# A graph-network kernel on one core: the column-number table of three wide comparisons moved from SBUF into a PSUM bank

## The chip, the core and the metric

The kernel runs on one core of one Trainium2 chip. A core has a matrix engine (PE, with its weight loads shown apart as PEld), a vector engine (DVE), a scalar engine (ACT), a general engine (POOL, also GpSimd) and a queue engine (SP); each works through its own list of instructions in order, and semaphores are the only ties between the lists. Data lie in SBUF, in PSUM (eight banks of 512 fp32 numbers per partition, written by PE, readable and writable by DVE and ACT) and in HBM. The metric is the time of one execution on the device in microseconds (us). The kernel before took 3636.62 us (median of 2 runs, 3635.95 to 3637.29).

## The reference

Four graph-network layers in a row on 6250 nodes of 128 features and 206250 edges sorted by target node. Only what bears on the change is shown:

```
def _L0_gnn_ref(x, edge_index, edge_attr, W, edge_w, b):
    src, dst = (edge_index[0], edge_index[1])
    xw = x @ W
    ew = edge_attr @ edge_w
    msg = xw[src] * ew
    out = jax.ops.segment_sum(msg, dst, num_segments=x.shape[0])
    return out + b
# layers 1 to 3: gather x[src], scale by degrees, segment_sum over dst, dense product
x = _layernorm(x + _L0_gnn_ref(...)); x = _layernorm(x + _L1_gnn_ref(...))
x = _layernorm(x + _L2_gnn_ref(...)); x = _layernorm(x + _L3_gnn_ref(...))
```

Layer 0 needs one row of `xw` per edge, multiplied by that edge's own product, and summed by target node. Layers 1 to 3 multiply node features by an adjacency matrix, which the kernel builds while layer 0 runs.

## The kernel before, in words

**Stages.** A short preparation computes `xw` and stores it in HBM. Then comes the **gather stage**, an unrolled loop of NH = 202 steps `n`, each for 8 tiles of 128 edges. Last come the dense layers, in which SP loads the stored adjacency matrix and PE multiplies.

**One step of the gather stage, engine by engine.**

- POOL issues 8 indirect DMAs (L563), each fetching 128 rows of `xw` into one of NG = 4 buffers of `gath`. Before step `n` it waits until step `n - 4` has been multiplied (`s_msg`). Every eighth step it issues one more indirect DMA (L547) for the edges of 256 target nodes.
- DVE, in this order: every eighth step `split_slots` (L631 to L642) turns edge words into pairs of small numbers; `hots(n - 4)` makes two comparison tables (L652: 16 tiles of 128 columns, L654: 16 tiles of 98 columns); `window_add(n - 1)` (L663) adds a PSUM result into `yT`; two multiplications (L677) form the messages from PSUM and `gath`; `window_hot(n + 1)` (L619) makes the comparison table of the next step, 8 tiles of 64 columns. Each comparison is a tensor_tensor `is_equal` of a table of column numbers with one number per tile and partition, broadcast.
- PE, in this order: every eighth step `turn_slots` (two transposes, L937); `a_products(n - 4)` (16 small products, L947, which ACT evicts from two PSUM banks); the message products (8 products, 16 records, L970) into bank 2 or 3 by turns; the edge products of the next step (2 products, 4 records, L930) into banks 0 and 1; `out_degrees` (4 products, L953).
- ACT copies the turned pairs (L1105) every eighth step and evicts four pairs of `a_products` per step (L1099). SP loads edge attributes and stores the adjacency blocks.

**Names.** `cols_key` and `cols_p` are the fp16 tables of column numbers (98 and 128 wide), `cols_pf` the fp32 one (128 wide); all lie in SBUF. `lokeyT` and `rel` are the numbers they are compared with, also in SBUF. `PB` is PSUM as eight banks; bank 7 holds the two turned places until ACT has copied them. The POOL instructions that make the tables are L529 to L531.

Of the kernel before, what the change touches and what calls it, by code (L numbers as in the profile page):

```python
# [14 lines left out]
F16 = mybir.dt.float16  # L15
# [9 lines left out]
P = 128  # L25
NB = -(-N // P)
NP = NB * P
T8 = 8
# [39 lines left out]
def build(nc, xT_d, x_d, ea_d, src_d, dst_d, next_d, edges_d, firstq_d, first16_d, half_d, w_d, vec_d, out_d):  # L68
    ctx = ExitStack()
    with ctx:  # L70
# [99 lines left out]
        first_edge = sb("first_edge", [P, NPB], I32)  # L170
        below = sb("below", [P, NPB, 3])
        pair_deg = sb("pair_deg", [P, NPB, 2])
        cols_key = sb("cols_key", [P, KW], F16)
        cols_p = sb("cols_p", [P, P], F16)
        cols_pf = sb("cols_pf", [P, P])
        flags = sb("flags", [P, 3])
        off_f = sb("off_f", [P, 1])
# [12 lines left out]
        g_block = msg[:, 0, :]  # L190

        PB = ctx.enter_context(nc.psum_tensor("pb", [P, 8, 512], F32))

        s_in = {n: sem("in_" + n) for n in ("w", "edge_w", "xT0", "xT1", "vecs", "src", "edges", "firsts", "rows", "x")}
        s_const = sem("consts_made")
# [323 lines left out]
        @block.gpsimd  # L519
        def _(pool):  # L520
            nc.gpsimd.iota(pair_dst[:, :], [[2 * P, NPB]], base=0, channel_multiplier=2, allow_small_or_imprecise_dtypes=True)
            nc.gpsimd.memset(edge_w[:, :, :], 0.0).then_inc(s_const, 1)
            nc.gpsimd.memset(ident[:, :], 0.0)
            nc.gpsimd.memset(x[:, NB - 1, :], 0.0).then_inc(s_const, 1)
            pool.wait_ge(s_const, 2)
            nc.gpsimd.affine_select(out=ident[:, :], in_=ident[:, :], compare_op=ALU.not_equal, fill=1.0,
                                    base=0, pattern=[[-1, P]], channel_multiplier=1)
            nc.gpsimd.memset(ones[:, :], 1.0)
            nc.gpsimd.iota(cols_key[:, :], [[1, NB], [NB, 2]], base=0, channel_multiplier=0, allow_small_or_imprecise_dtypes=True)  # L529
            nc.gpsimd.iota(cols_p[:, :], [[1, P]], base=0, channel_multiplier=0, allow_small_or_imprecise_dtypes=True)  # L530
            nc.gpsimd.iota(cols_pf[:, :], [[1, P]], base=0, channel_multiplier=0, allow_small_or_imprecise_dtypes=True)  # L531
            nc.gpsimd.iota(pair_key[:, :], [[KW * P, NPB]], base=0, channel_multiplier=KW, allow_small_or_imprecise_dtypes=True)
            nc.gpsimd.memset(flags[:, :], 0.0)
            nc.gpsimd.memset(g_deg[:, :, :], 0.0)
            nc.gpsimd.memset(eps_ln[:, 1:2], 1e-5)
            nc.gpsimd.memset(eps_ln[:, 3:4], 0.0)
            nc.gpsimd.iota(valid[:, :], [[0, 1]], base=0, channel_multiplier=1, allow_small_or_imprecise_dtypes=True).then_inc(s_const, 1)

            for b in range(NPB):
                if b % 5 == 0:  # L540
                    pool.wait_ge(s_q, b // 5 + 1)
                    pool.sem_inc(s_seen, 1)
                nc.gpsimd.indirect_dma_start(first16_i[:, b, :], None, first16_d,  # L543
                                             bass.IndirectOffsetOnAxis(ap=first_q[:, b:b + 1], axis=0)).then_inc(s_f16, 16)

            def slots_in(b):
                nc.gpsimd.indirect_dma_start(slots[:, b, :, :].rearrange("p e k -> p (e k)"), None, edges_d,  # L547
                                             bass.IndirectOffsetOnAxis(ap=first_edge[:, b:b + 1], axis=0)).then_inc(s_slot[b % 2], 16)

            pool.wait_ge(s_tab, 5)  # L550
            pool.wait_ge(s_rowxw, 2 * NT)
            pool.sem_inc(s_seen, 1)
            slots_in(0)
            pool.wait_ge(s_in["src"], 16)
            for h in range(2):
                pool.wait_ge(s_rowst[h], 16 * TURNS[h])
            pool.sem_inc(s_seen, 1)
            for n in range(NH):
                if n >= NG:
                    pool.wait_ge(s_msg, 2 * (n - NG) + 2)  # L560
                    pool.sem_inc(s_seen, 1)
                for t in range(n * T8, min(n * T8 + T8, ET)):
                    nc.gpsimd.indirect_dma_start(gath[:, T8 * (n % NG) + t % T8, :], None, xw_d,  # L563
                                                 bass.IndirectOffsetOnAxis(ap=src_i[:, t:t + 1], axis=0)).then_inc(s_gath[n % NG], 16)
                if n % BL == BL // 2 and n // BL + 1 < NPB:
                    slots_in(n // BL + 1)
            g_off = off(pool)
            general_pool(pool, 0, g_off)
            for k, bias in ((1, B_L1), (2, B_L2), (3, None)):
                Wk = s_walk[k]  # L570
                if k == 1:

                    pool.wait_ge(s_prep, NPB)

                def residual(t, s, p):
                    pool.wait_ge(Wk[f"xn{s}"], p + 1)
                    if k < 3:
                        nc.gpsimd.tensor_tensor(blocks(y, t), xn[s], vecs[:, bias, :].unsqueeze(1).broadcast_to([P, BT, D]), ALU.add).then_inc(Wk[f"yb{s}"], 1)  # L578
                    else:
                        pool.dma_start(x3_d[bass.ds(t * (BT * P), BT * P), :].rearrange("(b p) f -> p b f", p=P), xn[s]).then_inc(Wk[f"st{s}"], 16)  # L580

                walk(pool, residual)
                general_pool(pool, k, g_off)

            pool.wait_ge(s_x3, 16)
            nc.gpsimd.tensor_tensor(x3b, x3b, vecs[:, BN_BETA, :].unsqueeze(1).broadcast_to([P, NB, D]), ALU.add).then_inc(s_bn_pool, 1)  # L586

        @block.vector
        def _(v):
# [23 lines left out]
            nc.vector.tensor_scalar(first_edge[:, :], before_16[:, :], float(2 * FE), None, ALU.mult).then_inc(s_tab, 1)  # L613
            v.wait_ge(s_const, 3)
            nc.vector.tensor_copy(ident16[:, :], ident[:, :]).then_inc(s_tab, 1)  # L615

            def window_hot(n):
                at_tile = T8 * (n % 2)
                nc.vector.tensor_tensor(hot_win[:, at_tile:at_tile + T8, :], cols_pf[:, 0:WIN].unsqueeze(1).broadcast_to([P, T8, WIN]),  # L619
                                        rel[:, n * T8:n * T8 + T8].unsqueeze(2).broadcast_to([P, T8, WIN]), ALU.is_equal).then_inc(s_hotw, 1)  # L620

            cuts = [NPB + 1]
# [23 lines left out]
            def hots(j):  # L646
                b, c = j // BL, j % BL * NPR
                if j >= 2:
                    v.wait_ge(s_amm, GA * (j - 1))
                v.wait_ge(s_lk, b + 1)  # L650
                at_pair = NPR * (j % 2)
                nc.vector.tensor_tensor(hot_lo[:, at_pair:at_pair + NPR, :], cols_p[:, :].unsqueeze(1).broadcast_to([P, NPR, P]),  # L652
                                        lokeyT[:, b, c:c + NPR].unsqueeze(2).broadcast_to([P, NPR, P]), ALU.is_equal)
                nc.vector.tensor_tensor(hot_key[:, at_pair:at_pair + NPR, :], cols_key[:, :].unsqueeze(1).broadcast_to([P, NPR, KW]),  # L654
                                        lokeyT[:, b, P + c:P + c + NPR].unsqueeze(2).broadcast_to([P, NPR, KW]), ALU.is_equal).then_inc(s_hot, 1)

            def window_add(n):
# [254 lines left out]
        def _(pe):  # L912
# [18 lines left out]

            def turn_slots(b):
                pe.wait_ge(s_prep, b + 1)
                if b > 0:
                    pe.wait_ge(s_lk, b)
                for k in range(2):
                    last = nc.tensor.transpose(PB[:, 7, k * P:k * P + P], lo_key[:, k, :], ident[:, :])  # L937
                last.then_inc(s_tp, 1)

            def a_products(j):  # L940
# [19 lines left out]
            for n in range(NH):  # L960
                if n % BL == 2 and n // BL < NPB:
                    turn_slots(n // BL)
                if 0 <= n - LAG < NA:
                    a_products(n - LAG)
                pe.wait_ge(s_msg, 2 * n + 2)
                pe.wait_ge(s_hotw, n + 1)
                if n >= 2:
                    pe.wait_ge(s_add, n - 1)
                for t in range(T8):
                    last = nc.tensor.matmul(PB[:, 2 + n % 2, 0:WIN], msg[:, T8 * (n % 2) + t, :], hot_win[:, T8 * (n % 2) + t, :], start=(t == 0), stop=(t == T8 - 1))  # L970
                last.then_inc(s_win, 1)
                if n + 1 < NH:
                    edge_products(n + 1)
                if 0 <= n - LAG - 1 < NA:
                    out_degrees(n - LAG - 1)
            pe.wait_ge(s_off, 5)
            pe.wait_ge(s_lk, NPB)
            nc.tensor.matmul(PB[:, 7, 0:3], ones[:, :], flags[:, :], start=True, stop=True).then_inc(s_off, 1)
            pe.wait_ge(s_add, NH)
            g_off = off(pe)  # L980
# [96 lines left out]
        def _(act):  # L1077
# [24 lines left out]
            for n in range(NH):  # L1102
                if n % BL == 2 and n // BL < NPB:
                    act.wait_ge(s_tp, n // BL + 1)
                    nc.scalar.copy(lokeyT[:, n // BL, :], PB[:, 7, 0:2 * P]).then_inc(s_lk, 1)  # L1105
                if 0 <= n - LAG < NA:
                    evict(n - LAG)

# [134 lines left out]
```

## Time and profile before

| what | value |
|---|---|
| time, median of 2 runs | 3636.62 us |
| the profiled execution's own time | 3642.16 us |
| its span | 3639.8 us |
| PE busy | 2578.6 us (71%) |
| POOL busy | 2024.1 us (56%) |
| DVE busy | 1574.8 us (43%) |
| ACT busy | 530.3 us (15%) |
| indirect DMAs of the gather stage on POOL | 1612, from 58.8 to 2499.1 us |

The page gives busy times over the whole span. The gather stage fills about the first 2500 us and the dense layers the rest, and the two have different limits, so a share of the whole says little on either. In the lists, "idle before, releaser" tells how long an engine stood idle ahead of a group's instructions and what ended that; "issue" is time in which it waited for nothing that the profile shows. A matrix product of fp32 numbers shows as two records.

### The profile page before, as it was taken

What the parts mean: (1) busy time and instruction counts of PE and PEld (TensorE: products, weight loads), DVE (VectorE), ACT (ScalarE), POOL (GpSimd) and SP (SyncE); (2) the same over time, 40 slices, a digit from 0 to 9 for tenths busy, and PEclk for the clock granted to TensorE, in tenths of its full rate; (3) what the DMA queues carried; (4) which work ended last, traced back from release to release, by engine and by line L of the source; (5) the groups of instructions that cost most, each with busy time, mean ns of one, the idle gap of its engine ahead of it and who ended that gap; (6) DMA issues with size and microseconds to landing.
All of it is one profiled execution on the core that took longest, in us unless ns stands there. A gap on an engine that the chain in (4) does not pass through costs nothing.

```text
span 3639.8 us, 35592 instructions
## 1 busy us (share of the span) xinstructions
PE 2578.6 (71%) x12818; PEld 1594.3 (44%) x12818; DVE 1574.8 (43%) x2392; ACT 530.3 (15%) x1141; POOL 2024.1 (56%) x1703
## 2 busy tenths in 40 slices
PE   3566666766666666666667676765799899879980
PEld 2344444444444444444444444443444444545540
DVE  3455555455545454545454545454311311231136
ACT  0111111111111111111111111110200300111112
POOL 6777777777777777777777777773100200000001
PEclk7777777777777777777777777776899999889995
DMA  5222222222222222222222222226177577627641
GB/s 177 72 83 81 86 82 86 81 87 86 78 85 86 82 85 83 85 86 81 83 83 82 86 82 85 84 83 178 73 289 295 223 295 294 239 106 282 270 163 35
DMA packets 215777, 462.28 MB, mean 127 GB/s; under 512 B 43877, under 2 KB 84042, under 8 KB 215386
## 3 DMA queue, kind: packets, MB, share of 16 engines
q1 hardware_dynamic: 159358, 344.17, 25.4%
q0 software_dynamic: 54480, 112.65, 12.3%
q10 hardware_dynamic: 1804, 3.72, 0.3%
q8 instruction: 77, 1.26, 0.2%
q14 instruction: 58, 0.48, 0.0%
HBM read 372.09 MB, written 88.32 MB: 126 GB/s over the span
## 4 chain that ended last, share of the span: by engine, by line
POOL 51%; PE 25%; issue 16%; DVE 5%; another core or an unknown queue 1%; DMA 1%; ACT 1%; DVEq 0%; ACTq 0%; POOLq 0%; SPq 0%
POOL big L563 49%; PE pb L1032 11%; PE pb L1033 11%; PE pb L1007 1%; PE pb L1041 1%; POOL big L543 1%; POOL y L547 1%; DMA big<-at 0%; DVE y L886 0%; ACT tmp L1133 0%; PE pb L970 0%; DVE tmp L770 0%; DVE big L652 0%; PE pb L1057 0%
## 5 line engine op out<-in xcount | busy, mean ns | idle before, releaser
L563 POOL DMA_INDIRECT big<-xw,big x1612 | 1910.4, 1185 | 501.0 <-issue 490.9
L970 PE MATMUL pb<-big 128*128 128x64 f32 x3232 | 635.1, 378 | 638.8 <-DVE big L677 618.3
L970 PEld LDWEIGHTS pb<-big 128*128 128x128 f32 x3232 | 599.8, 286 | 671.6 <-DVE big L677 649.9
L677 DVE TENSOR_TENSOR big<-pb,big 128x512 f32<-128x512 f32 x404 | 261.3, 687 | 1103.5 <-DMA big<-xw,big 1059.0
L1032 PE MATMUL pb<-big,yT 128*128 128x512 f16 (+1 forms) x1911 | 688.0, 368 | 23.1 <-DMA big<-at 17.5
L930 PE MATMUL pb<-big 128*128 128x512 f32 x808 | 672.7, 982 | 24.4 <-DVE ident L615 24.4
L1033 PE MATMUL pb<-big,yT 128*128 128x512 f16 (+1 forms) x1911 | 687.8, 368 | 0.0
L1099 ACT CAST tmp<-pb 128x392 f16<-128x392 f32 x784 | 349.8, 488 | 1740.9 <-PE pb L947 1056.1
L652 DVE TENSOR_TENSOR big<-cols_p,big 128x2048 f16<-128x2048 f16 x196 | 447.9, 2285 | 0.8
L947 PE MATMUL pb<-big 128*128 128x98 f16 x3136 | 247.2, 212 | 173.7 <-ACT tmp L1099 80.8
L654 DVE TENSOR_TENSOR big<-cols_key,big 128x1568 f16<-128x1568 f16 x196 | 349.6, 1784 | 0.0
L930 PEld LDWEIGHTS pb<-big 128*128 128x128 f32 x808 | 235.3, 320 | 224.6 <-issue 224.6
L947 PEld LDWEIGHTS pb<-big 128*128 128x128 f16 x3136 | 176.2, 100 | 267.1 <-issue 124.7
L1032 PEld LDWEIGHTS pb<-big,yT 128*128 128x128 f16 x1911 | 187.5, 98 | 230.2 <-issue 26.7
L1033 PEld LDWEIGHTS pb<-big,yT 128*128 128x128 f16 x1911 | 187.4, 98 | 206.7 <-issue 2.5
L578 POOL TENSOR_TENSOR y<-tmp,vecs 128x896 f32 (+1 forms) x14 | 35.0, 2506 | 361.8 <-ACT tmp L1133 361.8
L828 DVE SCALAR_TENSOR_TENSOR y<-pb,small,y 128x128 f32 (+1 forms) x98 | 26.7, 344 | 460.5 <-PE pb L1041 460.5
L586 POOL TENSOR_TENSOR big<-big,vecs 128x6272 f32<-128x6272 f32 x1 | 13.4, 13387 | 341.5 <-DMA big<-x 341.5
L953 PEld LDWEIGHTS pb<-tmp,ident 128*128 128x128 f16 x784 | 91.7, 117 | 226.1 <-issue 205.2
L953 PE MATMUL pb<-tmp,ident 128*128 128x392 f16 x784 | 190.1, 371 | 0.0
L580 POOL DMA_DIRECT2D x<-tmp x7 | 6.7, 952 | 301.2 <-ACT tmp L1133 291.4
L619 DVE TENSOR_TENSOR big<-cols_pf,big 128x512 f32<-128x512 f32 x202 | 138.4, 685 | 0.0
(145 smaller groups left out, 1008.0 us busy)
## 6 DMA issues: line engine op xcount, KB each, us to landing
big<-at SPq DMA_DIRECT2D x36, 6272.0 KB, 18.0
at<-tmp SPq DMA_DIRECT2D x196, 392.0 KB
big<-xw,big POOLq DMA_INDIRECT x1612
big<-in_ea SPq DMA_DIRECT2D x202, 64.0 KB
big<-at SPq DMA_DIRECT2D x3, 1568.0 KB, 6.6
xw<-big SPq DMA_DIRECT2D x7, 448.0 KB
x<-tmp POOLq DMA_DIRECT2D x7, 448.0 KB, 7.3
out<-tmp SPq DMA_DIRECT2D x6, 448.0 KB, 3.0
```

The lines of the kernel that those rows point to most:

```text
L563: nc.gpsimd.indirect_dma_start(gath[:, T8 * (n % NG) + t % T8, :], None, xw_d, bass.IndirectOffsetOnAxis(ap=src_i[:, t:t + 1], axis=0)).th ...
L619: nc.vector.tensor_tensor(hot_win[:, at_tile:at_tile + T8, :], cols_pf[:, 0:WIN].unsqueeze(1).broadcast_to([P, T8, WIN]), rel[:, n * T8:n ...
L652: nc.vector.tensor_tensor(hot_lo[:, at_pair:at_pair + NPR, :], cols_p[:, :].unsqueeze(1).broadcast_to([P, NPR, P]), lokeyT[:, b, c:c + NPR ...
L654: nc.vector.tensor_tensor(hot_key[:, at_pair:at_pair + NPR, :], cols_key[:, :].unsqueeze(1).broadcast_to([P, NPR, KW]), lokeyT[:, b, P + c ...
L677: nc.vector.tensor_tensor(msg[:, T8 * (n % 2) + 4 * q:T8 * (n % 2) + 4 * q + 4, :], PB[:, q, :].rearrange("p (t f) -> p t f", f=D), gath[: ...
L930: nc.tensor.matmul(PB[:, q, :], ea[:, n % NG, :], edge_w[:, 4 * q:4 * q + 4, :], start=True, stop=True).then_inc(s_ew, 1)
L947: last = nc.tensor.matmul(PB[:, 4 + g % 2, i * KW:i * KW + KW], hot_lo[:, at_pair, :], hot_key[:, at_pair, :], start=True, stop=True)
L953: last = nc.tensor.matmul(PB[:, 6, 0:NB * T8], ident16[:, :], stage[:, j % 2, :].rearrange("p (h d) -> p h d", d=SN)[:, :, g * T8:g * T8 + ...
L970: last = nc.tensor.matmul(PB[:, 2 + n % 2, 0:WIN], msg[:, T8 * (n % 2) + t, :], hot_win[:, T8 * (n % 2) + t, :], start=(t == 0), stop=(t = ...
L1032: nc.tensor.matmul(PB[:, c, 0:n], parts_v[0][:, b, :], piece, start=(b == 0), stop=False)
L1033: last = nc.tensor.matmul(PB[:, c, 0:n], parts_v[1][:, b, :], piece, start=False, stop=(b == NB - 1))
L1099: nc.scalar.copy(stage[:, j % 2, :].rearrange("p (h d) -> p h d", d=SN)[:, :, c:c + 2 * GP].rearrange("p h (i a) -> p h i a", a=2), PB[:, ...
```

## The change

The two fp16 tables become one fp32 table in PSUM, 226 columns of bank 7: DVE copies `cols_pf` and `cols_key` (now fp32) there once, before the first step. The three comparisons read it. The general path, which these inputs don't take, still reads `cols_pf` in SBUF. The turned places lie in columns 64 to 319 of bank 2 instead, beside the message products' 64 columns. The waits are changed with that: `turn_slots` waits for the addition that last read bank 2, the message products of every eighth step wait for ACT's copy of the turned places, and the three-column product at the end, which goes to bank 7, waits until all comparisons are done.

```diff
-        cols_key = sb("cols_key", [P, KW], F16)
-        cols_p = sb("cols_p", [P, P], F16)
+        cols_key = sb("cols_key", [P, KW])
         cols_pf = sb("cols_pf", [P, P])
...
         PB = ctx.enter_context(nc.psum_tensor("pb", [P, 8, 512], F32))
+        cols = PB[:, 7, 0:P + KW]
...
-            nc.gpsimd.iota(cols_p[:, :], [[1, P]], base=0, channel_multiplier=0, allow_small_or_imprecise_dtypes=True)
...
             nc.vector.tensor_copy(ident16[:, :], ident[:, :]).then_inc(s_tab, 1)
+            nc.vector.tensor_copy(cols[:, 0:P], cols_pf[:, :])
+            nc.vector.tensor_copy(cols[:, P:P + KW], cols_key[:, :]).then_inc(s_tab, 1)
+            v.wait_ge(s_tab, 7)
...
-                nc.vector.tensor_tensor(hot_win[:, at_tile:at_tile + T8, :], cols_pf[:, 0:WIN].unsqueeze(1).broadcast_to([P, T8, WIN]),
+                nc.vector.tensor_tensor(hot_win[:, at_tile:at_tile + T8, :], cols[:, 0:WIN].unsqueeze(1).broadcast_to([P, T8, WIN]),
...
-                nc.vector.tensor_tensor(hot_lo[:, at_pair:at_pair + NPR, :], cols_p[:, :].unsqueeze(1).broadcast_to([P, NPR, P]),
+                nc.vector.tensor_tensor(hot_lo[:, at_pair:at_pair + NPR, :], cols[:, 0:P].unsqueeze(1).broadcast_to([P, NPR, P]),
...
-                nc.vector.tensor_tensor(hot_key[:, at_pair:at_pair + NPR, :], cols_key[:, :].unsqueeze(1).broadcast_to([P, NPR, KW]),
+                nc.vector.tensor_tensor(hot_key[:, at_pair:at_pair + NPR, :], cols[:, P:P + KW].unsqueeze(1).broadcast_to([P, NPR, KW]),
...
             def turn_slots(b):
                 pe.wait_ge(s_prep, b + 1)
-                if b > 0:
-                    pe.wait_ge(s_lk, b)
+                pe.wait_ge(s_add, b * BL + 1)
                 for k in range(2):
-                    last = nc.tensor.transpose(PB[:, 7, k * P:k * P + P], lo_key[:, k, :], ident[:, :])
+                    last = nc.tensor.transpose(PB[:, 2, WIN + k * P:WIN + k * P + P], lo_key[:, k, :], ident[:, :])
...
                     pe.wait_ge(s_add, n - 1)
+                if n % BL == 2 and n // BL < NPB:
+                    pe.wait_ge(s_lk, n // BL + 1)
...
-            pe.wait_ge(s_lk, NPB)
+            pe.wait_ge(s_hotw, NH)
+            pe.wait_ge(s_hot, NA)
...
-                    nc.scalar.copy(lokeyT[:, n // BL, :], PB[:, 7, 0:2 * P]).then_inc(s_lk, 1)
+                    nc.scalar.copy(lokeyT[:, n // BL, :], PB[:, 2, WIN:WIN + 2 * P]).then_inc(s_lk, 1)
```

## Rows read from the trace of the kernel before

**Rows 1.** The page: the span in 40 slices, POOL busy and TensorE clock, in tenths

```profile
POOL 6777777777777777777777777773100200000001
PEclk7777777777777777777777777776899999889995
```

**Rows 2.** The page: chain that ended last, shares of the span by line

```profile
POOL big L563 49%; PE pb L1032 11%; PE pb L1033 11%; PE pb L1007 1%; PE pb L1041 1%; POOL big L543 1%; POOL y L547 1%; DMA big<-at 0%; DVE y L886 0%; ACT tmp L1133 0%; PE pb L970 0%; DVE tmp L770 0%; DVE big L652 0%; PE pb L1057 0%
```

**Rows 3.** The page: costliest groups; busy us, mean ns of one, idle before

```profile
L563 POOL DMA_INDIRECT big<-xw,big x1612 | 1910.4, 1185 | 501.0 <-issue 490.9
...
L677 DVE TENSOR_TENSOR big<-pb,big 128x512 f32<-128x512 f32 x404 | 261.3, 687 | 1103.5 <-DMA big<-xw,big 1059.0
...
L652 DVE TENSOR_TENSOR big<-cols_p,big 128x2048 f16<-128x2048 f16 x196 | 447.9, 2285 | 0.8
...
L654 DVE TENSOR_TENSOR big<-cols_key,big 128x1568 f16<-128x1568 f16 x196 | 349.6, 1784 | 0.0
...
L619 DVE TENSOR_TENSOR big<-cols_pf,big 128x512 f32<-128x512 f32 x202 | 138.4, 685 | 0.0
```

**Rows 4.** Line L563: duration ns min/median/max, first and last start

```profile
L563 POOL DMA_INDIRECT big<-xw,big x1612: 942/947/2964, 58.8 to 2499.1; - x180
```

**Rows 5.** Timeline, an issue with DVE idle: start us, us, what [idle before]

```profile
60.05 0.95 POOL L563 DMA_INDIRECT big<-xw,big  x1 [0.30 <-issue]
```

**Rows 6.** Timeline of one step in the middle, POOL and DVE

```profile
1504.68 1.29 DVE L677 TENSOR_TENSOR big<-pb,big 128x512 f32<-128x512 f32 x2 [6.14 <-DMA big<-xw,big]
1505.79 0.95 POOL L563 DMA_INDIRECT big<-xw,big  x1 [0.31 <-issue]
1505.88 0.68 DVE L619 TENSOR_TENSOR big<-cols_pf,big 128x512 f32<-128x512 f32 x1
...
1506.48 2.29 DVE L652 TENSOR_TENSOR big<-cols_p,big 128x2048 f16<-128x2048 f16 x1
1507.04 2.55 POOL L563 DMA_INDIRECT big<-xw,big  x1 [0.30 <-issue]
1508.68 1.78 DVE L654 TENSOR_TENSOR big<-cols_key,big 128x1568 f16<-128x1568 f16 x1
...
1509.89 1.40 POOL L563 DMA_INDIRECT big<-xw,big  x1 [0.30 <-issue]
1510.39 0.21 DVE L663 TENSOR_TENSOR yT<-yT,pb 128x64 f32 x1
```

**Rows 7.** Timeline of PE: a step at the low clock, a step at the high one

```profile
1107.26 3.67 PE L970 MATMUL pb<-big 128*128 128x64 f32 x16 [6.37 <-DVE big L677]
...
1116.70 0.74 PE L947 MATMUL pb<-big 128*128 128x98 f16 x8 [0.47 <-issue]
...
156.21 1.96 PE L970 MATMUL pb<-big 128*128 128x64 f32 x16
...
162.78 1.96 PE L970 MATMUL pb<-big 128*128 128x64 f32 x16
```

**Rows 8.** Stretches: PE, PEld, DVE, ACT, POOL busy, then clock, DMA share, GB/s

```profile
137.00:170.00 33.00, 27.07 (x188) 18.04 (x188) 32.00 (x32) 7.78 (x18) 27.08 (x20) 0.95 0.32 99
...
1000.00:1500.00 500.00, 338.83 (x1677) 224.27 (x1678) 256.41 (x304) 76.92 (x173) 398.15 (x335) 0.73 0.29 84
```

**Rows 9.** Groups by shape: busy us, mean ns of one, idle before

```profile
L547 POOL DMA_INDIRECT y<-in_edges,first_edge x25 | 23.7, 948 | 13.2 <-issue 7.3 <-DVE ident L615 5.9
...
L1105 ACT CAST big<-pb 128x256 f16<-128x256 f32 x25 | 9.3, 373 | 353.0 <-PE pb L937 181.1 <-remote 151.5 <-issue 20.4
...
L636 DVE SCALAR_TENSOR_TENSOR tmp<-y,tmp 128x128 f32<-128x128 int32 x25 | 7.8, 313 | 0.0
L698 DVE TENSOR_TENSOR x<-x,vecs 128x896 f32<-128x896 f32 x7 | 7.6, 1085 | 0.0
```

**Rows 10.** Timeline of the start, DVE's last preparation and first multiplication

```profile
56.62 0.22 DVE L615 CAST ident<-ident 128x128 f16<-128x128 f32 x1
...
70.21 1.29 DVE L677 TENSOR_TENSOR big<-pb,big 128x512 f32<-128x512 f32 x2 [12.77 <-DMA big<-xw,big]
```

## The prediction, made before the changed kernel had run

> **What bounds the kernel now.** I read four views in this order. The page's slices show two regimes: POOL is busy at seven tenths for about 28 of 40 slices and then nearly silent, with the TensorE clock at 0.7 to 0.8 first and 0.9 after [rows 1]. The chain of waits puts 49% of the span on one POOL line, L563, and 11% on each of the two dense products [rows 2]. So the gather stage ends when POOL has issued its 1612 indirect DMAs, and only that stage is touched by the change. The costliest groups then give the shape of the bound: L563 is busy 1910.4 us, 1185 ns a piece, and the idle time ahead of it is 490.9 us of "issue", 0.30 us a piece, with almost nothing that another engine releases. DVE, for its part, stands idle for 1059.0 us until gathered rows land [rows 3]. Nobody holds POOL up by a semaphore; it is slow by itself.
>
> The line's own view says how slow. The median issue is 947 ns and the shortest 942, while the mean is 1185 and the longest 2964 [rows 4]. With DVE idle an issue takes 0.95 us and the next comes 0.30 us later [rows 5], so eight of them would be 10.0 us a step. The stage takes (2499.1 - 58.8) / 201.5 = 12.1 us a step [rows 4] (the last step has 4 issues).
>
> The timeline of a step shows where 2.1 us go [rows 6]. The issue of 1507.04 begins inside the comparison L652 (1506.48 to 1508.77) and takes 2.55 us: it ends at 1509.59, 0.82 us after the comparison. The one of 1509.89 begins inside L654 (ending 1510.46) and takes 1.40: it ends at 1511.29, 0.83 after. The one of 1505.79 begins inside the second multiplication of L677 (1504.68 to 1505.97) and takes 0.95: nothing is added. L677 reads one operand in PSUM and one in SBUF; L652 and L654 read both in SBUF. My reading: an issue that needs SBUF while DVE reads two SBUF operands stands still until DVE is done, then needs its last 0.82 us.
>
> **The change, part by part.**
>
> 1. *Three comparisons read their table in PSUM.* With one SBUF operand left they are of L677's kind, so I take the whole added time away. 1612 issues at the median 0.947 are 1526.6 us; measured are 1910.4 [rows 3, 4]; excess 383.8 us. Not all of it goes. Two-SBUF instructions that the change leaves are the seven additions L698 (1.09 us each) and the pair steps of `split_slots` (25 times 0.31 for L636, with one more like it beside it) [rows 9]. An issue caught by one of the seven loses at most 1.09 + 0.82 - 0.95 = 0.96 us, seven of them 6.7 us; the short ones lose at most 0.2, fifty of them 10. As most won't fall so, I keep 6 us and take **378 us** off. Bounds: 384 if nothing is left, 367 if all fall badly.
>
> 2. *What the comparisons themselves cost.* The nearest row is L677 against L619, both 128x512 fp32, the one from PSUM and the other from SBUF alone: 687 and 685 ns [rows 3]. L652 and L654 in fp16 lie on L619's line, (2285 - 685) / (2048 - 512) = 1.04 ns an element, so fp16 buys nothing that an fp32 table would lose. I take 2 ns each, off the path: DVE waits 6.14 us a step for rows to land [rows 6]. Without that cover 594 comparisons would cost 1.2 us.
> [...]
>
> 3. *PE's bank 2.* `turn_slots` now waits for the addition of step 8b, which DVE's list has ahead of the split that it waited for already: nothing. The message products of step 8b + 2 wait for ACT's copy, 0.37 us [rows 9]; between the two PE does `a_products`, whose ACT evictions come behind that copy in ACT's list, so only the first of the 25 (no `a_products` yet) may pay 0.4 us, at a step where POOL is four buffers ahead. The last product waits for comparisons that were done before the message products ahead of it: nothing.
>
> 4. *Start.* One iota on POOL goes, ahead of a wait for DVE: nothing. Two copies on DVE come in; L615 is the nearest, 0.22 us [rows 10], so 0.5 us, ahead of a multiplication that waits 12.77 us for its rows [rows 10]. With no cover, 0.5.
>
> **Does POOL stay the bound?** At 10.0 us a step others come close.
> DVE: 1.29 + 0.68 + 2.29 + 1.78 + 0.21 = 6.25 us [rows 6]. Far.
> PE: its list closes on itself, since every product of a step needs the one before. [...] POOL needs a buffer back only after three further steps, 30 us, which evens single slow steps out.
>
> **The sum.** The profiled execution's own time is 3642.16, 5.5 over the median of the runs, 3636.62. 3642.2 - 378 = 3264; the same against the median is **3259 us**, 10.4% less. The dense layers are not touched.
>
> **The rivals.**
>
> *A. PE becomes the bound (0.07).* If the clock stays low, a PE step costs 10.2 to 10.6 us (the upper end where `out_degrees` is slow as well), 0.2 to 0.6 above POOL's, times 196: 39 to 118 us given back, 3300 to 3375. [...]
>
> *B. The port is not the cause, or PSUM doesn't free it (0.04).* The two long comparisons are also the longest DVE instructions and write the most. If writing holds POOL up, nothing changes: 3637. Against it: L677 writes as well, and adds nothing [rows 6].
> [...]
>
> *C. DVE becomes the bound, and the kernel slower (0.02).* If reading a broadcast table in PSUM slows the three comparisons by a factor r, DVE's step is 1.50 + 4.75 r. It passes POOL's 10.0 at r = 1.8 and today's 12.1 at r = 2.2; at r = 3 it is 15.8, 3.7 above today's times 196, some 4360 us. Nothing speaks for it but that no row has an fp32 PSUM operand beside an fp16 one or with a repeated column range; L677 speaks against it.
>
> *D. Half the gain (0.03).* The comparisons still block for a part, or gathers at a steady 10.0 us a step meet slower landings: half of 378 is 3448.
>
> **How the numbers follow.** Forecast 0.84. Its own range is 3252 (384 off) to 3272 (367 off, and a few us of clock in the dense layers either way), widened by a slow PE step here and there. With the lower part of A the range is 3245 to 3310; outside lie B, C, D, most of A. About 2% is what a measurement of this kernel can tell from no change: all but B and C are faster by more. Faster 0.94, same 0.04, slower 0.02.
>
> **What the changed profile would show.** Right: L563's mean within 10 ns of 947, its longest under 2 us, its last start at 2499 - 378 = 2121 us, a step of 10.0 us, the three comparisons within 10 ns of now, DVE's wait for rows about 4 us a step. Steps above 10.0 with message products that start right behind `a_products`, and a clock near 0.5, would be A. Issues that still end 0.82 us after a comparison would be B. Comparisons of double length would be C. The forecast is wrong too if POOL shows idle time released by L677, the sign that a buffer comes back late.

## The result: slower by 3.8%, and the profile after

| | before | after |
|---|---|---|
| median | 3636.62 us | 3775.78 us (3774.11 to 3777.45) |
| ratio to before | | 1.0383, interval 1.0338 to 1.0427 |
| span of the profiled execution | 3639.8 us | 3772.0 us |
| POOL busy | 2024.1 us | 1640.0 us |
| last indirect DMA of the stage starts at | 2499.1 us | 2618.9 us |

Forecast were 3259 us and a last issue at 2121 us. POOL lost 384 us of work, and the stage became 120 us longer. The span grew by 132.2 us: 119.8 until the last issue, 12.4 behind it.

The page of the changed kernel, in the order of parts 2, 4 and 5, answers to [rows 1], [rows 2] and [rows 3]:

```profile
POOL 6566666556556556655655655564100100000001
PEclk6666677677666767667776766677699999979995
...
PE 44%; another core or an unknown queue 31%; issue 12%; ACT 7%; DVE 4%; DMA 1%; ACTq 1%; DVEq 0%; POOL 0%; SPq 0%; POOLq 0%
...
L562 POOL DMA_INDIRECT big<-xw,big x1612 | 1526.6, 947 | 1005.0 <-DVE big L679 554.5
...
L665 DVE TENSOR_TENSOR yT<-yT,pb 128x64 f32 x202 | 43.6, 216 | 1141.1 <-remote 1105.9
L654 DVE TENSOR_TENSOR big<-pb,big 128x2048 f16<-128x2048 f32 x196 | 447.1, 2281 | 0.8
L679 DVE TENSOR_TENSOR big<-pb,big 128x512 f32<-128x512 f32 x404 | 269.2, 687 | 200.8 <-PE pb L932 153.2
L656 DVE TENSOR_TENSOR big<-pb,big 128x1568 f16<-128x1568 f32 x196 | 348.7, 1779 | 0.0
```

The issue L562 fell from 1185 to 947 ns, as forecast, and the comparisons cost what they did. But POOL now stands idle for 554.5 us until a multiplication gives a buffer back (10.1 us before, in the full row of this line), the multiplication no longer waits for rows, and DVE spends 1105.9 us ahead of the addition L665, released by "remote". POOL's share of the chain that ended last is 0%; 31% of it is "another core or an unknown queue". Both words say that the view found no instruction whose end explains the release. There is one core, so that is a thing to look into, and the timeline shows it. A step of the changed kernel, all engines:

```profile
1491.94 0.53 PE L948 MATMUL pb<-big 128*128 128x98 f16 x8
...
1492.40 0.49 ACT L1103 CAST tmp<-pb 128x392 f16<-128x392 f32 x1 [6.87 <-PE pb L954]
...
1492.94 0.35 PE L948 MATMUL pb<-big 128*128 128x98 f16 x4 [0.47 <-issue]
...
1494.87 0.48 ACT L1103 CAST tmp<-pb 128x392 f16<-128x392 f32 x1 [1.98 <-remote]
...
1495.41 0.35 PE L948 MATMUL pb<-big 128*128 128x98 f16 x4 [2.11 <-issue]
...
1495.60 1.96 PE L973 MATMUL pb<-big 128*128 128x64 f32 x16
...
1497.40 3.61 PE L932 MATMUL pb<-big 128*128 128x512 f32 x4
...
1498.39 0.49 ACT L1103 CAST tmp<-pb 128x392 f16<-128x392 f32 x1 [3.04 <-remote]
...
1502.67 0.48 ACT L1103 CAST tmp<-pb 128x392 f16<-128x392 f32 x1 [3.79 <-PE pb L948]
...
1504.31 0.94 POOL L562 DMA_INDIRECT big<-xw,big  x1 [0.30 <-issue]
1508.51 0.33 SPq L465 DMA_DIRECT2D big<-in_ea  x1
1508.53 0.22 DVE L665 TENSOR_TENSOR yT<-yT,pb 128x64 f32 x1 [11.87 <-remote]
1508.67 1.28 DVE L679 TENSOR_TENSOR big<-pb,big 128x512 f32<-128x512 f32 x2
1508.71 0.87 ACT L1103 CAST tmp<-pb 128x392 f16<-128x392 f32 x2 [5.56 <-remote]
1509.25 0.90 PE L948 MATMUL pb<-big 128*128 128x98 f16 x8 [5.01 <-ACT tmp L1103]
...
1510.73 0.94 POOL L562 DMA_INDIRECT big<-xw,big  x1 [5.48 <-DVE big L679]
```

The addition L665 waits for the message products L973. Those end at 1497.56; the addition starts at 1508.53, 11.0 us later, with DVE idle. SP waits for the edge products L932, which end at 1501.01, and goes on at 1508.51. ACT goes on at 1508.71. So three engines that wait for PE alone, for products that ended at different times, are released within 0.2 us of each other. By the profile the products are done (a product's end is modelled there, but the products behind L973 had started too); what is late, then, is their **completion signal**. The trace has a record of semaphore updates besides, and it agrees: the update by the message products stands at 1508.41, those by the edge products at 1508.45 and 1508.49, while DVE's update for its next multiplication stands at 1509.36, right at that instruction's end.

The addition's late signal (1508.41) arrives 3.2 us after POOL's last issue ends (1505.25), and POOL had stopped because its four buffers were full: it waits for the multiplication, which is behind the addition on DVE, which waits for the signal.

ACT's copies show what happens before POOL stops. The four copies of this step start at 1492.40, 1494.87, 1498.39 and 1502.67, which is 0.1, 2.4, 5.1 and 6.9 us after the ends of their products, while POOL was issuing without a pause. So signals do come through while POOL issues, but each later than the one before.

POOL therefore issues for two steps (20 us), stands for 5.5, and begins again: 12.7 us a step on average ((2618.9 - 58.5) / 201.5), against 12.1 before.

**The sign was in the trace before.** Its start has a stretch in which no comparison blocks POOL yet, steps 0 to 5. The timeline of the kernel before, there:

```profile
86.94 3.67 PE L970 MATMUL pb<-big 128*128 128x64 f32 x16 [8.39 <-DVE big L677]
...
118.85 0.94 POOL L563 DMA_INDIRECT big<-xw,big  x1 [0.30 <-issue]
...
126.23 0.22 DVE L663 TENSOR_TENSOR yT<-yT,pb 128x64 f32 x1 [36.79 <-remote]
...
129.63 0.94 POOL L563 DMA_INDIRECT big<-xw,big  x1 [9.83 <-DVE big L677]
```

The message products of step 1 end at 90.6, and their addition starts 35.6 us later, after POOL had run out of buffers; its last issue had ended 6.4 us before (119.79). I read these rows for the start alone and took the wait for one of its transfers. Nor was every signal prompt later on, when the comparisons did block POOL. In the middle of the stage before the change:

```profile
960.30 2.00 PE L970 MATMUL pb<-big 128*128 128x64 f32 x16 [1.92 <-DVE big L677]
...
969.24 0.95 POOL L563 DMA_INDIRECT big<-xw,big  x1 [0.30 <-issue]
...
969.86 0.22 DVE L663 TENSOR_TENSOR yT<-yT,pb 128x64 f32 x1 [2.99 <-remote]
```

The addition starts 7.6 us after the products' end, and POOL is issuing then, so an arriving signal needs no full stop of POOL. Such waits are few there: the addition waited 65.7 us for "remote" in the whole run, against 1105.9 after the change.

### The profile page after: what moved, and what is told of

The parts are those of the page before. It is cut to its first block, busy times and chain, and to the rows that moved or that the text cites. A ratio compares the mean times of both kernels' runs of the same rounds, so it can differ in the third digit from the quotient of the medians.

```text
span 3772.0 us, 35619 instructions
## 1 busy us (share of the span) xinstructions
PE 2520.3 (67%) x12818; PEld 1563.0 (41%) x12818; DVE 1574.8 (42%) x2394; ACT 541.0 (14%) x1141; POOL 1640.0 (43%) x1702
## 4 chain that ended last, share of the span: by engine, by line
PE 44%; another core or an unknown queue 31%; issue 12%; ACT 7%; DVE 4%; DMA 1%; ACTq 1%; DVEq 0%; POOL 0%; SPq 0%; POOLq 0%
PE pb L1036 10%; PE pb L1037 10%; PE pb L932 7%; PE pb L973 7%; ACT tmp L1103 6%; PE pb L948 5%; PE pb L954 2%; PE pb L1011 1%; PE pb L1045 1%; ACT tmp L1137 1%; DMA big<-at 0%; DVE y L888 0%; DVE tmp L772 0%; PE pb L1061 0%
## 5 line engine op out<-in xcount | busy, mean ns | idle before, releaser
L562 POOL DMA_INDIRECT big<-xw,big x1612 | 1526.6, 947 | 1005.0 <-DVE big L679 554.5
L948 PE MATMUL pb<-big 128*128 128x98 f16 x3136 | 301.2, 230 | 950.3 <-ACT tmp L1103 489.0
L1103 ACT CAST tmp<-pb 128x392 f16<-128x392 f32 x784 | 361.3, 487 | 2073.6 <-remote 1115.6
L948 PEld LDWEIGHTS pb<-big 128*128 128x128 f16 x3136 | 199.5, 108 | 1069.9 <-ACT tmp L1103 534.9
L973 PE MATMUL pb<-big 128*128 128x64 f32 x3232 | 600.0, 363 | 55.1 <-DVE big L679 54.8
L932 PE MATMUL pb<-big 128*128 128x512 f32 x808 | 619.8, 912 | 24.3 <-DVE ident L614 24.3
L973 PEld LDWEIGHTS pb<-big 128*128 128x128 f32 x3232 | 572.1, 274 | 66.1 <-DVE big L679 61.5
L665 DVE TENSOR_TENSOR yT<-yT,pb 128x64 f32 x202 | 43.6, 216 | 1141.1 <-remote 1105.9
L654 DVE TENSOR_TENSOR big<-pb,big 128x2048 f16<-128x2048 f32 x196 | 447.1, 2281 | 0.8
L656 DVE TENSOR_TENSOR big<-pb,big 128x1568 f16<-128x1568 f32 x196 | 348.7, 1779 | 0.0
L932 PEld LDWEIGHTS pb<-big 128*128 128x128 f32 x808 | 213.7, 291 | 201.1 <-issue 201.1
```

The costliest lines, as they stand in the source:

```text
L665: nc.vector.tensor_tensor(where, where, PB[:, 2 + n % 2, 0:WIN], ALU.add).then_inc(s_add, 1)
L932: nc.tensor.matmul(PB[:, q, :], ea[:, n % NG, :], edge_w[:, 4 * q:4 * q + 4, :], start=True, stop=True).then_inc(s_ew, 1)
L948: last = nc.tensor.matmul(PB[:, 4 + g % 2, i * KW:i * KW + KW], hot_lo[:, at_pair, :], hot_key[:, at_pair, :], start=True, stop=True)
L1103: nc.scalar.copy(stage[:, j % 2, :].rearrange("p (h d) -> p h d", d=SN)[:, :, c:c + 2 * GP].rearrange("p h (i a) -> p h i a", a=2), PB[:, ...
```

## The experiments

Theory 1, formed from these rows: **PE's completion signals arrive late while POOL issues indirect DMAs without a break. The two-SBUF comparisons used to make the breaks**, one of about 1.6 us and one of about 0.45 us a step (2.55 and 1.40 us less the usual 0.95 [rows 6]), and the change took them away. Theory 2: the shared bank 2, or the new waits, cost the time. Theory 3: reading the table in PSUM delays PE's signals.

### First group: which part, which cause

The edits below are abridged. `undo_table`, the changed kernel with the three comparisons on SBUF again:

```diff
-  hot_win <- cols[:, 0:WIN];  hot_lo <- cols[:, 0:P];     hot_key <- cols[:, P:P + KW]
+  hot_win <- cols_pf[:, 0:WIN]; hot_lo <- cols_pf[:, :];  hot_key <- cols_key[:, :]
```

> The changed kernel, but the three comparisons read their tables in SBUF again (both fp32); bank 2 for the turned places and the changed waits stay. Theory 1 (PE's completion signals arrive late while POOL issues indirect DMAs without a break; the comparisons used to make the breaks): POOL's mean issue is back at about 1185 ns, PE's signals are prompt again, 3637 us within 10. Theory 2 (a product or a copy in bank 2, or the new waits, cost the time): stays near 3776 or gets worse, since the old issue times come on top. Theory 3 (reading the table in PSUM delays PE's signals) also expects 3637 here.

`short_tables`, from the kernel before, where the two wide comparisons make one tile of 16 (so the adjacency matrix is not the right one):

```diff
+                made = NPR if j < 2 else 1
-  hot_lo[:, at_pair:at_pair + NPR, :] and hot_key[:, at_pair:at_pair + NPR, :]
+  hot_lo[:, at_pair:at_pair + made, :] and hot_key[:, at_pair:at_pair + made, :]
```

> The kernel before, with its tables in SBUF, but the two wide comparisons of each step make one tile of 16 from the third step on (the other 15 keep the first steps' numbers, so the adjacency matrix is not the reference's). DVE neither blocks POOL for long nor reads a table in PSUM. Theory 1: POOL issues without breaks again, PE's signals come late, steps of 10.0 and about 15 us in turn, 3720 to 3800 us although DVE has 3.8 us less to do in a step. Theory 3: no table is read in PSUM, so signals are prompt and POOL sets 10.0 us a step, 3260 us.

`pause_four`, from the changed kernel: four memsets on POOL between the fourth and the fifth gather of a step (`pause_one` has 1 in place of 4):

```diff
                 for t in range(n * T8, min(n * T8 + T8, ET)):
+                    for _ in range(4 if t % T8 in (4,) else 0):
+                        pool.wait_ge(s_idle, paused)
+                        nc.gpsimd.memset(idle_room[:, :], 0.0).then_inc(s_idle, 1)
+                        paused += 1
```

> The changed kernel with one break in POOL's issues per step: four memsets of 384 columns, some 2 us, between the fourth and the fifth gather. Theory 1: the break lets PE's signals through as the comparisons did, a step is 10.0 + 2.0 to 2.3 us, 3620 to 3700 us, less than the changed kernel although POOL has more to do. Theory 3: signals stay late, since the table is still in PSUM, and the added POOL work makes it no faster than 3776.

> The same with one memset, some 0.5 us of break per step. Theory 1 leaves open how long a break must be: if 0.5 us is enough, a step is 10.6 us and the time about 3380 us, better than both kernels; if not, between 3400 and 3776. Theory 3: 3776 or more.

Measured: undo_table 3640.23 us, ratio 1.0006 (0.9994 to 1.0019). short_tables 3774.43 us, 1.0379 (1.0346 to 1.0413). pause_four 3591.15 us, 0.9871 (0.9855 to 0.9888). pause_one 3762.82 us, 1.0349 (1.0332 to 1.0366).

undo_table falls back to the old time with bank 2 and the new waits in place: theory 2 is out. short_tables is the one that separates 1 from 3. It reads no table in PSUM, DVE has 3.5 us less to do in a step (2285 and 1784 ns against 285 and 254 for the short forms), and it is as slow as the changed kernel. The groups of short_tables, its POOL issues and its two comparisons (the means include the two full-size ones of the first steps):

```profile
L563 POOL DMA_INDIRECT big<-xw,big x1612 | 1545.1, 958 | 976.4 <-DVE big L678 528.5 <-issue 447.9
...
L653 DVE TENSOR_TENSOR big<-cols_p,big 128x128 f16<-128x128 f16 (+1 forms) x196 | 59.9, 306 | 0.8
L655 DVE TENSOR_TENSOR big<-cols_key,big 128x98 f16<-128x98 f16 (+1 forms) x196 | 52.9, 270 | 0.0
```

The issues are near 947 ns (958) and the idle time behind full buffers is back at 528.5 us. Theory 3 is out as the cause. pause_four adds work to the engine that sets the pace, and is faster than both kernels, and than the 3620 us that I gave as its lower bound; its groups and one step:

```profile
L569 POOL DMA_INDIRECT big<-xw,big x1612 | 1528.0, 948 | 461.2 <-issue 461.2
...
L567 POOL MEMSET idle_room<- 128x384 f32 x804 | 339.8, 423 | 34.8
...
L672 DVE TENSOR_TENSOR yT<-yT,pb 128x64 f32 x202 | 42.8, 212 | 57.4 <-remote 38.0 <-PE pb L980 19.3
```

```profile
1502.25 3.67 PE L980 MATMUL pb<-big 128*128 128x64 f32 x16 [2.27 <-DVE big L686]
...
1504.29 1.87 POOL L567 MEMSET idle_room<- 128x384 f32 x4
...
1506.31 0.95 POOL L569 DMA_INDIRECT big<-xw,big  x1 [0.16 <-issue]
1506.61 0.21 DVE L672 TENSOR_TENSOR yT<-yT,pb 128x64 f32 x1
```

No idle time is left that a multiplication ends, and the addition waits 57.4 us in all instead of 1141.1. In the step, the message products end at 1505.92 and the addition starts 0.7 us later, as soon as DVE is through with its comparison. POOL is the bound again, at 11.7 us in most steps.

### Second group: how long a break must be

> The changed kernel with two memsets of 384 columns on POOL per step, about 0.85 us more between the fourth and the fifth gather (four gave 1.7 us and 3591 us, one gave 0.29 us and 3763 us). If 0.85 us is enough for PE's signals, a step is 10.0 + 0.85 us and the time 3420 us; if the signals still come late, it lies between 3591 and 3763.

> The same with three memsets, about 1.3 us more. If enough, 10.0 + 1.3 us a step and 3505 us, faster than both kernels and than four memsets; if not, above 3591.

`pause_spread` has one memset where `t % T8 in (1, 3, 5, 7)`, `pause_alternate` has four where `t % (2 * T8) == 4`.

> Four memsets per step again, but one after every second gather, so POOL issues as seldom as with the four in one place, and no break is longer than 0.6 us (0.3 us is usual). If PE's signals need a lower mean rate of issues, 3591 us or less, as with the four together. If they need one long break, they come late in spite of the same POOL work: steps of 15 us among those of 11.2, 3700 us or more.

> Four memsets in one place, but only in every second step. If a 2 us break every 21.7 us lets the waiting signals through in time, a pair of steps takes 21.7 us and the time is about 3430 us; if a break is needed in every step, a step of 15 us comes back for each one without a break, and it is 3650 us or more.

The break is the time from the end of the fourth issue to the start of the fifth, read from each timeline (0.30 us with no memset); the idle time is that of the issue's group which the multiplication ends.

| kernel | longest break in a step | POOL idle for a buffer | time, ratio to before (interval) |
|---|---|---|---|
| changed | 0.30 us | 554.5 us | 3775.78, 1.0383 (1.0338 to 1.0427) |
| pause_one | 0.59 | 465.1 | 3762.82, 1.0349 (1.0332 to 1.0366) |
| pause_two | 1.07 | 342.1 | 3780.61, 1.0369 (1.0322 to 1.0416) |
| pause_three | 1.54 | 198.4 | 3716.03, 1.0211 (1.0160 to 1.0261) |
| pause_four | 2.01 | 0 | 3591.15, 0.9871 (0.9855 to 0.9888) |
| pause_spread | 4 of 0.59 | 253.6 | 3715.62, 1.0192 (1.0163 to 1.0221) |
| pause_alternate | 2.0, every second step | 309.3 | 3802.22, 1.0437 (1.0406 to 1.0468) |

My hope of 3420 or 3505 us with a shorter break failed, and pause_two came out above the 3763 us that I had as its upper end. A break of 0.6 us gains 13 us on the changed kernel and one of 1.1 us nothing, one of 1.5 us gains 60 us, and 2.0 us in every step keeps the signals prompt almost throughout; in every second step it gains nothing. pause_spread has POOL do the same work as pause_four and is 125 us slower, so the rate of issues alone is not what counts. It is 60 us faster than the changed kernel, so neither is the length alone.

### Third group: issues, bytes or landings, and one comparison at a time

> The changed kernel with the widest comparison (16 tiles of 128 columns) reading its table in SBUF again, the other two in PSUM. An issue caught by it stands still for about 1.6 us per step, a break like that of the four memsets, and the 0.45 us that the other wide comparison cost are saved. Theory 1 (a break of that length lets PE's signals through): steps of 11.6 us, 3637 - 196 x 0.45 = 3549 us, faster than both kernels. If the PSUM reads that remain were at fault: 3700 us or more.

> The other way round: only the comparison of 16 tiles of 98 columns reads its table in SBUF. It begins behind the widest one and now an issue that starts inside it stands still for up to 1.7 us, one that starts near its end for 0.1. Theory 1: between 3590 and 3790 us, by how long the break turns out to be; late signals if it is under 1.3 us, prompt ones if it is 1.6.

`narrow_rows` gathers `[..., 0:WIN]` from `xw` seen as rows of 64. `sp_rows`:

```diff
+                if n >= 1 and n - 1 + NG < NH:
+                    sp.wait_ge(s_msg, 2 * n)
+                    rows_in(n - 1 + NG)     # 8 x sp.dma_start(gath tile, 128 rows of xw_d)
...
-                for t in range(n * T8, min(n * T8 + T8, ET)):     # POOL's indirect DMAs
+                for t in range(n * T8, 0):
```

> The changed kernel with gathers that fetch 64 instead of 128 columns from the fifth step on (the other half of each message is an earlier step's, so layer 0 is not the reference's): half the bytes, as many issues. If PE's signals wait for the issues, nothing changes: steps of 10.0 and 15 us in turn, 3760 to 3790 us. If they wait for the gathered bytes on their way, they come earlier: fewer than half of the 15 us steps, under 3700 us.

> The changed kernel with the rows of each step fetched by eight plain DMAs from SP's queue instead of eight indirect ones from POOL (rows in order of place, so layer 0 is not the reference's): the same bytes and landings, no issue on POOL in the stage but one in eight steps. Theory 1 (the issues on POOL hold PE's signals back): signals are prompt, PE or SP sets the step at 7 to 9 us, 2600 to 3000 us. If the landings or the bytes hold them back, signals stay late, as many as in the changed kernel.

Measured: lo_in_sbuf 3621.88 us, 0.9949 (0.9935 to 0.9963); key_in_sbuf 3681.93 us, 1.0118 (1.0101 to 1.0136); narrow_rows 3768.44 us, 1.0356 (1.0324 to 1.0387); sp_rows 2444.17 us, 0.6717.

Half the bytes change nothing, so the bytes are not it; as many gathers landed, so landings are not ruled out by that run. With the issues gone from POOL, as many bytes and eight DMAs landing per step as before, PE's signals are prompt. So neither bytes nor landings as such delay them. But sp_rows changes the engine that issues, its queue and the kind of DMA together, and doesn't tell which of the three counts. The groups of sp_rows and one of its steps:

```profile
L676 DVE TENSOR_TENSOR yT<-yT,pb 128x64 f32 x202 | 42.4, 210 | 11.9 <-PE pb L984 11.9
```

```profile
804.26 1.28 DVE L690 TENSOR_TENSOR big<-pb,big 128x512 f32<-128x512 f32 x2
...
810.08 1.28 DVE L690 TENSOR_TENSOR big<-pb,big 128x512 f32<-128x512 f32 x2
```

A step is 5.8 us, the addition waits 11.9 us in the whole run, and the tables are read in PSUM all the while, which clears them a second time. My 2600 to 3000 us was too high: DVE, not PE or SP, sets that pace; from 200 to 1200 us it is busy for 981.5 of 1000 us, and PE for 891.7. This kernel is no version to use, since it fetches rows in order.

lo_in_sbuf keeps one former break, 1.6 us long (with the usual 0.3, a gap of 1.9, just under that of pause_four), and is 18 us faster than the kernel before, where I had expected 88: 45.1 us of POOL's idle time still wait for a buffer. key_in_sbuf, with the other comparison's break, has 234.6 us. Its issues took 1711.5 us, 0.94 us a step over the 1526.6 of the changed kernel, so that break is shorter.

### Fourth group: the place, and a break on demand

`gate` has POOL do `pool.wait_ge(s_win, n - 1)` between the fourth and the fifth gather; `pause_first` has the four memsets where `t % T8 in (0,)`.

> The changed kernel, where POOL waits between the fourth and the fifth gather of step n until the message products of step n - 2 are signalled. With prompt signals that has long happened and costs nothing; with late ones POOL stops at once, not only when its four buffers are full. If a stop must last some 3.1 us until late signals arrive, as in the changed kernel, whatever the stop is made of, and each step of the stage needs one, a step is 13 us and the time 3800 us or more; if a stop clears the way for a step or two behind it, a pair of steps takes 20.0 + 3.1 us and it is 3560 us.

> The four memsets (3591 us between the fourth and the fifth gather) ahead of the first gather of a step instead. If only the length of the break counts, 3591 us within 15, with steps of 11.7 us. If it counts what PE does during it, the time differs, up to the 3776 us of no break.

Measured: pause_first 3606.62 us, 0.9908 (0.9890 to 0.9926): the place counts 15 us, the length 185. gate 3690.46 us, 1.0145 (1.0127 to 1.0163), 85 us faster than the changed kernel and 99 us slower than pause_four: it lies between my two cases. So stopping POOL until the signal is there gains less than a fixed break does.

## Why the prediction was wrong, step by step

1. **The added time of the issues: right within 6 us.** 1612 issues at 947 ns, 1526.6 us, against 1910.4: 384 us less where I took off 378. undo_table has them at 1182 ns again. The two-SBUF instructions that stay add about 5 us over the median of 944 ns (1526.6 less 1612 x 0.944), where I had kept 6; the longest issue took 2.38 us (the second row below), not under 2: it began inside one of the four flag instructions of steps 6 to 9 (208.19 to 210.02 us), which I had left out, and ended 0.82 us after it, as the issues of [rows 6] do. Rival B falls: the issues took 1185 ns with the three comparisons' tables in SBUF and 947 with them in PSUM, while the two long comparisons took as long either way (point 2). That it is a port for which an issue waits, as that rival's name has it, no run shows.
2. **The comparisons: right.** 2281 and 1779 ns from PSUM, 2285 and 1784 before; none got longer. Rival C falls.
3. **Bank 2 and the waits: right**, at nothing (undo_table 1.0006).
4. **The start: right.** The first issue is at 58.5 instead of 58.8 us.
5. **"Does POOL stay the bound?": this step failed.** I priced PE's step by the times of its products and took for granted that a product's end reaches those who wait for it at once. I counted 30 us of slack from four buffers, but the message products' signals came some 11 us late in every second step, and POOL stood idle for 554.5 us, waiting for buffers. Whether more buffers would have helped was not tried. The stall I removed as a loss was also what kept another path open, and it was the cheaper of the two: 2.05 us a step, against 2.7 for full buffers.
6. Rival A named PE as the next bound for its speed, and that is not what happened: in the changed stage PE is idle for 38% of the time, at a granted clock of 0.70 (the first row below) against the 0.73 of [rows 8]. Its 10.2 us a step is one step of [rows 7], from 1107.26 to the end of the last `a_products` at 1117.44; the clock was 0.50 under that step's message products (1107.3 to 1110.9 us) and 0.58 over the whole of it. A stage that stays at the low clock, with steps of 10.2 to 10.6 us and the 39 to 118 us worked out from them, no run shows; in its place most steps of the changed kernel take 10.0 and some 15 us in turn, as POOL finds its buffers full. The chance of 0.02 for slower was worked out from rivals that I had priced, with none for a coupling between engines that share no data. Semaphores are not all that ties the lists: with no semaphore between them, an issue of 0.95 us took 2.55 beside L652 [rows 6].

The rows for points 6 and 1, of the changed kernel: first the busy time of PE, its weight load, DVE, ACT and POOL in a stretch of 500 us, with the granted clock behind them; then the shortest, median and longest issue in ns:

```profile
1000.00:1500.00 500.00, 311.57 (x1594) 207.20 (x1594) 246.79 (x293) 73.61 (x162) 302.59 (x321) 0.70 0.27 80
```

```profile
L562 POOL DMA_INDIRECT big<-xw,big x1612: 938/944/2382, 58.5 to 2618.9; - x180
```

The sign that I had put down for a wrong forecast, idle time of POOL released by the multiplication, is the one that appeared.

**Open.** By what path POOL's issues hold back PE's signals, whether it is the issue itself, POOL's queue or the landings of its gathers, and why 1.5 us of break is too little and 2.0 enough, no run shows. Since the ends of products are modelled, the trace doesn't tell a signal sent late from products whose last writes were late. Nor is it shown why pause_first is 15 us slower than pause_four. DVE's and ACT's own signals are not seen to be late: the multiplication of 1508.67 and its issue of 1510.73 follow DVE's work at once, and ACT's copy at 1508.71 releases PE at 1509.25. Whether other engines' signals would be late with other loads wasn't tried.

## What to carry to other kernels

Before removing a stall from the engine that sets the pace, look in the same trace for a stretch where it already runs without the stall, and follow every other engine through that stretch, not only the one at issue. Releases marked "remote" or "unknown queue" on a single core can mean, as here, that a signal came later than the work it reports: compare the end of the work with the start of the one who waited. Where a POOL that issues indirect DMAs shares a loop with PE, measure a deliberate break in the issues; here 2.0 us in every step was worth 185 us against none and 48 us against the accidental breaks.

## What the hardware did that I had not expected

- By the records of semaphore updates, the message products' signal came 35.5 us after their modelled end in step 1 of the kernel before (90.61 to 126.11 us); in the changed kernel the addition started about 11 us after that end in every second step, while POOL issued an indirect DMA every 1.25 us. In the changed kernel the message products' signal came 3.1 us after the last issue's end in the median of POOL's stops (2.7 to 8.1), at the start of the kernel before 6.3 us; some signals to ACT came through before POOL stopped.
- An issue that starts inside one of the wide DVE comparisons of two SBUF operands ends 0.82 us after it, whichever part of the comparison it started in (392 of 394 such issues in the kernel before; the other two started within 0.02 us of the comparison's start and took 0.95). With one operand in PSUM the issues inside the comparisons took 0.96 us at most.
- One engine made to do 340 us more of memsets gave a kernel that is 185 us faster.
